# Second attention: one transfer for the turned maximum from SP's queue, rows stored tile by tile

## The chip, the cores and the metric

The kernel runs on one core of a Trainium2 chip. The metric is the time of one execution on the device in microseconds; the time before is 1258.41 us, the median of three runs (1256.88 to 1260.72).

## The reference

The input is x, 8 x 512 rows of 512 numbers, and a context of 8 x 120 rows. Four layers follow, each with a layernorm in front and a residual behind: a cross-attention with one head, a quantised linear layer, a second cross-attention with 16 heads of 32, and a mixture of experts with one shared and eight routed feed-forward networks. The change lies in the second attention:

```python
q = (query @ w_q.T).reshape(B, T_q, N_HEADS, HEAD_DIM)
k = (kv_source @ w_k.T).reshape(B, T_kv, N_HEADS, HEAD_DIM)
v = (kv_source @ w_v.T).reshape(B, T_kv, N_HEADS, HEAD_DIM)
attn = softmax(einsum('bqhd,bkhd->bhqk', q, k) * HEAD_DIM ** (-0.5), axis=-1)
out = einsum('bhqk,bkhd->bqhd', attn, v).reshape(B, T_q, D_MODEL) @ w_o.T
x = x + out
```

## The kernel before

The rows are worked on in 32 tiles of 128 (four to a batch element). The program runs four stages one after the other, each a set of five generators, one for each engine queue: the first attention with the quantised layer (`front`), the second attention (`attention1`), the shared network (`shared`) and the experts (`experts`). `both` in `stages` weaves them: the table JOIN says after which step of the first stage a part of a step of the second is issued, and the table TAIL says after which part (4 x step + part) of the second stage's last steps the first pieces of the shared network are issued.

In `attention1` a step t works on several tiles at once. TensorE makes the scores of tile t (four groups c of four heads, line L1510), and VectorE takes the maximum of each group (L1260). The maxima, split in a high and a low part (L1267, L1269), are turned by TensorE (L1517) and copied by ScalarE into `shiftT` (32 rows of 128, `shift_copied`, L1422). A transfer lays them as two more rows (96 and 97) under the packed queries of the tile, `g.queries[t % 3]`. One step later the turned scores of the tile (`scores_transposed`, L1537) are made from packed keys and packed queries with these rows, so that the maximum comes off in the same product. ScalarE's exponentials follow (L1391, L1395, L1402), GpSimd makes low parts (L1217), TensorE the outputs (L1553 to L1555), the output is turned (L1560) and goes through the output product (`product(t - 3, k)` in four quarters, L1606). The queries of tile t + 2 are made by `queries` (L124 is the helper `matmuls`).

Transfers: SP writes the queries of tile t + 1 to `q_rows` (L1184), waits until they landed, and reads them back packed with three loads (`packed_queries`, by the helper `spread`, L133). It stores the normed rows of tile t - 4 to `xn_rows` (L1188) and their turned form to `xt_tiles` (L1197). Every fourth step it stores four tiles of the residual rows to `x_rows` (L1204, 1 MB). Every fourth step it loads packed keys (also L133). ScalarE's queue issues the transfer of the turned maximum, in two halves of 4 KB (`shift_rows`, L1428), behind the exponentials of group 3. `n_in` counts these landings: TensorE waits for it ahead of the first turned scores, ScalarE ahead of the next copy.

An engine issues its instructions in the order in which the generators give them; a wait for a semaphore holds everything behind it on that engine.

## Time and profile before

| | us |
|---|---|
| median of three runs | 1258.41 |
| profiled execution | 1257.52 |
| its span | 1255.7 |
| TensorE (PE) busy | 1175.9 |
| VectorE (DVE) busy | 934.9 |
| ScalarE (ACT) busy | 664.5 |
| GpSimd (POOL) busy | 538.9 |
| second attention, some 32 tiles | about 250 to 620 |

Times in the trace are microseconds from the span's start. PEld is TensorE's weight load, which runs beside its matmuls; a name with q (SPq, ACTq) is an instruction of the engine's queue alone, such as the issue of a transfer. A number in square brackets at the end of a timeline's line is the idle time of the engine before it, with what ended it. The end of a matmul is modelled, so its start is the safer number.

### The profile page before, as it was taken

Reading aid. Unit: us, or ns where it says so; the run is one execution under the profiler, and the core shown is the slowest. Engines: PE = TensorE matmul, PEld = TensorE weight load, DVE = VectorE, ACT = ScalarE, POOL = GpSimd, SP = SyncE. Lnnn points to the kernel's source line nnn. Section 1 sums busy time; section 2 is a strip of 40 time slices with the busy share of each in tenths; the row PEclk is TensorE's granted clock in tenths of the full one; section 3 lists DMA queues with packets and bytes.
Section 4 is the critical chain, followed back from the end, with each engine's and each line's share of the span. In section 5 each row is a group of like instructions: output and inputs, shape, how many; then the busy total and the mean of one; then the engine's idle time right before and its main releaser. Section 6 shows DMA issues by size and latency. Waiting matters only on the chain.

```text
span 1255.7 us, 28634 instructions
## 1 busy us (share of the span) xinstructions
PE 1175.9 (94%) x10724; PEld 800.9 (64%) x10724; DVE 934.9 (74%) x2080; ACT 664.5 (53%) x1199; POOL 538.9 (43%) x682
## 2 busy tenths in 40 slices
PE   6888998679999999997899999999999999999996
PEld 3555655567777787875444444677777777666663
DVE  5899897878898898886586777777677776645450
ACT  4377787567788787775454322122222232465652
POOL 0057667644444444432200000364555455277744
PEclk9999999999999999999999999999999999999999
DMA  9522023123445444562791050304121503599987
GB/s 343 213 68 69 1 33 45 43 75 119 164 152 165 165 154 167 169 178 78 214 182 34 1 168 1 102 2 102 23 80 35 168 23 106 161 254 240 262 137 97
DMA packets 159608, 150.49 MB, mean 120 GB/s; under 512 B 80592, under 2 KB 113520, under 8 KB 159472
## 3 DMA queue, kind: packets, MB, share of 16 engines
q1 hardware_dynamic: 138432, 121.75, 33.6%
q0 software_dynamic: 14400, 25.35, 9.9%
q10 hardware_dynamic: 6640, 1.58, 0.7%
q8 instruction: 86, 1.41, 0.5%
q14 instruction: 50, 0.41, 0.1%
HBM read 84.93 MB, written 57.19 MB: 113 GB/s over the span
## 4 chain that ended last, share of the span: by engine, by line
PE 78%; DVE 8%; DMA 6%; issue 3%; ACT 2%; POOL 2%; ACTq 0%; SPq 0%; DVEq 0%; POOLq 0%
PE bank L124 28%; PE bank L2241 15%; PE bank L2234 13%; PE bank L1606 6%; DMA att_land<-att_land 4%; PE bank L980 3%; PE bank L1537 3%; PE bank L1560 2%; PE bank L1510 2%; PE bank L1049 1%; DMA q_rows<-att_land 1%; PE bank L897 1%; DMA att_land<-q_rows 1%; DVE front_amax L793 1%; PE bank L916 1%
## 5 line engine op out<-in xcount | busy, mean ns | idle before, releaser
L1739 POOL DMA_INDIRECT lists<-att_land x128 | 135.5, 1058 | 287.6 <-DVE att_land L1880 168.8
L2234 PE MATMUL bank<-att_land 128*128 128x512 f16 x768 | 176.2, 379 | 0.0
L124 PE MATMUL bank<-program_xs,program_wgu 128*128 128x512 f16 x576 | 128.9, 379 | 0.6 <-DVE att_land L1839 0.6
L2062 ACT ACTIVATE att_land<-program_x 128x512 f32<-128x512 f32 x40 | 25.2, 631 | 195.2 <-DVE program_x L2204 195.2
L2234 PEld LDWEIGHTS bank<-att_land 128*128 128x128 f16 x768 | 75.1, 98 | 81.7
L1217 POOL TENSOR_TENSOR att_land<-att_land 120x512 f16<-120x512 f32 x64 | 74.2, 1159 | 92.5 <-ACT att_land L1402 92.5
L124 PE MATMUL bank<-att_land 128*128 128x128 f16 (+1 forms) x1560 | 106.0, 221 | 3.0 <-DVE att_land L1323 3.0
L1260 DVE TENSOR_REDUCE bank<-bank 128x4 f32<-128x480 f32 x128 | 84.8, 662 | 30.9 <-PE bank L1510 29.5
L1606 PE MATMUL bank<-att_land 128*128 128x512 f16 x384 | 104.0, 383 | 1.7 <-DVE att_land L1344 1.7
L124 PEld LDWEIGHTS bank<-program_xs,program_wgu 128*128 128x128 f16 x576 | 56.0, 98 | 67.3 <-DVE att_land L1839 1.1
L124 PEld LDWEIGHTS bank<-att_land 128*128 128x128 f16 x1560 | 89.3, 98 | 5.9 <-DVE att_land L1323 3.5
L2241 PE MATMUL bank<-program_x 128*128 128x256 f16 x720 | 85.1, 273 | 0.0
L2403 POOL DMA_INDIRECT out_rows<-program_x,att_land x40 | 69.9, 1747 | 34.5 <-ACT program_x L2444 19.5
L124 PE MATMUL bank<-program_x 128*128 128x256 f16 (+2 forms) x504 | 80.5, 318 | 0.6 <-DVE program_x L2496 0.6
L1402 ACT ACTIVATE att_land<-bank 120x512 f16<-120x512 f32 x128 | 76.7, 599 | 8.0 <-PE bank L1537 5.0
L2013 ACT ACTIVATE att_land<-att_land 128x512 f16<-128x512 f32 x64 | 40.3, 629 | 74.2 <-PE bank L2234 34.5
L2241 PEld LDWEIGHTS bank<-program_x 128*128 128x128 f16 x720 | 70.5, 98 | 8.1
L451 POOL TENSOR_TENSOR program_x<-program_x,att_land 128x512 f32<-128x512 f32 x32 | 40.8, 1276 | 75.8 <-ACT att_land L569 75.8
L2073 DVE TENSOR_TENSOR att_land<-att_land 128x512 f16<-128x512 f32 x64 | 43.9, 686 | 33.2 <-ACT att_land L2013 33.1
L124 PE MATMUL bank<-program_wgu,att_land 128*128 128x120 f16 (+1 forms) x480 | 52.2, 253 | 16.6 <-DVE att_land L770 13.9
L124 PEld LDWEIGHTS bank<-program_x 128*128 128x128 f16 x504 | 49.2, 98 | 28.9 <-DVE program_x L2496 1.1
L2241 PE MATMUL bank<-program_xs,program_wgu 128*128 128x256 f16 x480 | 65.6, 273 | 0.0
(322 smaller groups left out, 2967.7 us busy)
## 6 DMA issues: line engine op xcount, KB each, us to landing
xn_rows<-att_land SPq DMA_DIRECT2D x37, 256.0 KB, 2.9
out_rows<-att_land SPq DMA_DIRECT2D x37, 256.0 KB, 7.2
att_land<-q_rows SPq DMA_DIRECT2D x66, 128.0 KB, 2.6
q_rows<-att_land SPq DMA_DIRECT2D x32, 256.0 KB, 2.1
xt_tiles<-att_land SPq DMA_DIRECT2D x32, 256.0 KB, 2.1
x_rows<-program_x SPq DMA_DIRECT2D x8, 1024.0 KB, 4.8
att_land<-x_rows SPq DMA_DIRECT2D x8, 1024.0 KB, 5.5
program_xs<-xt_tiles SPq DMA_DIRECT2D x28, 256.0 KB, 5.4
```

What stands on the lines that cost most here:

```text
L124: last = pe.matmul(out, lhs(a, k), rhs(b, k), start=n == 0, stop=n == len(terms) - 1)
L451: pool.tensor_tensor(g.x[:, u, :], g.x[:, u, :], y[:, u % 2], ALU.add).then_inc(a["x_new"], 1)
L1217: pool.tensor_tensor(pT[0:J, c, 1], prob[0:J, c], pT[0:J, c, 0], ALU.subtract).then_inc(c4["p_lo"], 1)
L1260: dve.tensor_reduce(nmax[:, c], ps_s[:, :, :], AX.X, ALU.max, negate=True).then_inc(c4["max"], 1)
L1402: act.activation(pT[0:J, c, 0], ps_t[c % 2][0:J, :], ACT.Exp).then_inc(c4["p_hi"], 1)
L1606: last = pe.matmul(ps_y[:, :], oT[:, u % 2, a, k, :], g.wo1[:, b, k, :], start=k == 0 and n == 0, stop=k == KC - 1 and n == 2)
L1739: pool.indirect_dma_start(out=io["lists"], out_offset=bass.IndirectOffsetOnAxis(ap=index[:, t, k:k + 1], axis=0), in_=load[:, t, k, :], in ...
L2013: act.activation(hid[:, v % 2, 0], hf[:, v % 2], ACT.Copy).then_inc(s["h_hi"].handle, 1)
L2073: tt(hid[:, v % 2, 1], hf[:, v % 2], hid[:, v % 2, 0], ALU.subtract).then_inc(s["h_lo"].handle, 1)
L2234: last = pe.matmul(ps_y[i][:, :], hid[:, c % 2, a, i * P:(i + 1) * P], wd[:, q, c, :], start=c == 0 and n == 0, stop=c == NC - 1 and n == 2)
L2241: last = pe.matmul(out, lhs(a, k), rhs(q, k), start=n == 0, stop=n == len(terms) - 1)
L2403: pool.indirect_dma_start(out=io["out"], out_offset=bass.IndirectOffsetOnAxis(ap=lst[:, u * CT + n, 0:1], axis=0), in_=res[:, c, n, :], in ...
```

## The change

Six things. On SP, the store of `xn_rows` moves from between the write of `q_rows` and the packed loads to behind these loads. The store of `x_rows` is made for each tile, in the step in which its `xn_rows` is stored, instead of for four tiles every fourth step. The transfer of the turned maximum is issued by SP behind these two, as one transfer of 32 rows, after a wait for ScalarE's copy; ScalarE's `shift_rows` is gone, and `n_in` counts 16 a tile instead of 32. On TensorE, the first turned scores (group 0) come behind the first quarter of the output product and the scores of group 1 instead of ahead of both, and the second ones (group 1) behind the third quarter instead of ahead of it. The shared network's wait for the stored rows counts 32 stores. In TAIL, the first piece of the shared network on TensorE goes in behind part 3 of step 31 instead of part 2.

```diff
--- before.py
+++ after.py
@@ -1183,9 +1183,6 @@
                 sp.wait_ge(s["q_lo"], u + 1)
                 sp.dma_start(io["q_rows"][u], qT[:, :, :, :].rearrange("p q k n -> p q (k n)")).then_inc(q_out[u % 2], 16)
             v = t - 4
-            if live(v):
-                sp.wait_ge(lg.ok, v + 1)
-                sp.dma_start(io["xn_rows"][v * P:(v + 1) * P, :], lg.xn[:, v % 2]).then_inc(rows_out[v % 2], 16)
             if live(u):
                 sp.wait_ge(q_out[u % 2], 16 * (u // 2 + 1))
                 need(sp, c4["t_mm"], KC * (u - 2))
@@ -1193,15 +1190,17 @@
                     sp.wait_ge(f.a["sim"], NT)
                 packed_queries(sp, g, io, u, q_in)
             if live(v):
+                sp.wait_ge(lg.ok, v + 1)
+                sp.dma_start(io["xn_rows"][v * P:(v + 1) * P, :], lg.xn[:, v % 2]).then_inc(rows_out[v % 2], 16)
+                sp.wait_ge(s["x_new"], v + 1)
+                sp.dma_start(io["x_rows"][v * P:(v + 1) * P, :], g.x[:, v, :]).then_inc(g.x_out.handle, 16)
+            if live(t):
+                sp.wait_ge(s["n_ok"], t + 1)
+                sp.dma_start(g.queries[t % 3][COPIES * DH:ROWS].rearrange("p r (c n) -> p (r c) n", n=P),
+                             shiftT[0:2 * HEADS, :]).then_inc(n_in, 16)
+            if live(v):
                 sp.wait_ge(s["g_lo"], v + 1)
                 sp.dma_start(io["xt_tiles"][v, :, :], gT[:, v % 2].rearrange("p q k n -> p (q k n)")).then_inc(gt_out[v % 2], 16)
-
-            if t >= TB and t % TB == 0:
-                b = t // TB - 2
-                if b >= 0:
-                    sp.wait_ge(s["x_new"], TB * (b + 1))
-                    rows = io["x_rows"][b * S:(b + 1) * S, :].rearrange("(i p) n -> p i n", p=P)
-                    sp.dma_start(rows, g.x[:, b * TB:(b + 1) * TB, :]).then_inc(g.x_out.handle, 16)
 
         def finish():
             for n in range(2):
@@ -1418,15 +1417,8 @@
         def shift_copied(u):
             if live(u):
                 act.wait_ge(s["n_mm"], u + 1)
-                need(act, n_in, 32 * u)
+                need(act, n_in, 16 * u)
                 act.activation(shiftT[0:2 * HEADS, :], ps_n, ACT.Copy).then_inc(s["n_ok"], 1)
-
-        def shift_rows(u):
-            if live(u):
-                act.wait_ge(s["n_ok"], u + 1)
-                for q in range(2):
-                    act.dma_start(g.queries[u % 3][COPIES * DH + q:COPIES * DH + q + 1].rearrange("p r (c n) -> p (r c) n", n=P),
-                                  shiftT[q * HEADS:(q + 1) * HEADS, :]).then_inc(n_in, 16)
 
         def query_high(u):
             if live(u):
@@ -1480,7 +1472,6 @@
             shift_copied(t)
             yield
             exps(t - 1, 3)
-            shift_rows(t)
             gate_high(t - 4)
             weights_high(t)
             if t == NT - 6:
@@ -1522,7 +1513,7 @@
                 return
             b = u // TB
             if c == 0:
-                pe.wait_ge(n_in, 32 * (u + 1))
+                pe.wait_ge(n_in, 16 * (u + 1))
                 if u % TB == 0 and b < 2:
                     pe.wait_ge(ones, b + 1)
             if u == 0 and c == 0:
@@ -1631,13 +1622,13 @@
         def step(t):
             scores(t, 0)
             rows_transposed(t + 2)
+            product(t - 3, 0)
+            yield
+            scores(t, 1)
             scores_transposed(t - 1, 0)
-            product(t - 3, 0)
-            yield
-            scores(t, 1)
             product(t - 3, 1)
+            product(t - 3, 2)
             scores_transposed(t - 1, 1)
-            product(t - 3, 2)
             yield
             scores(t, 2)
             product(t - 3, 3)
@@ -1963,7 +1954,7 @@
                     sp.dma_start(io["out"][bass.ds(((b - 1) * TB + i) * P, P), :], res[:, i]).then_inc(out_done.handle, 16)
             if b < B:
                 if b == 0:
-                    need(sp, g.x_out, 16 * B)
+                    need(sp, g.x_out, 16 * NT)
                     need(sp, t.y_mm, NT)
                 need(sp, out_done, 16 * TB * b)
                 sp.dma_start(res[:, :, :], io["x_rows"][b * S:(b + 1) * S, :].rearrange("(i p) n -> p i n", p=P)) \
@@ -2610,7 +2601,7 @@
         "gpsimd": [],
         "scalar": [135, 137, 142, 143],
         "vector": [135, 139, 150],
-        "tensor": [126, 130, 134, 139, 143, 147]}
+        "tensor": [127, 130, 134, 139, 143, 147]}
 
 
 def stages(nc, g, io):
```

## Rows read from the trace of the kernel before

**Rows 1.** The page's chain of work that ended last, by engine.
```profile
PE 78%; DVE 8%; DMA 6%; issue 3%; ACT 2%; POOL 2%; ACTq 0%; SPq 0%; DVEq 0%; POOLq 0%
```
**Rows 2.** Windows: length, busy time (instructions) by engine; clock, DMA share, GB/s.
```profile
454.76:464.83 10.07, 10.07 (x163) 8.53 (x161) 9.53 (x23) 8.77 (x16) 4.28 (x8) 1.00 0.49 160
443.53:454.76 11.23, 10.27 (x163) 8.50 (x161) 9.73 (x23) 8.24 (x15) 5.59 (x10) 1.00 0.50 153
```
**Rows 3.** Waits of TensorE's weight loads, 270 to 585: total, times, longest.
```profile
PEld bank L1537 <- DMA att_land<-att_land: 12.3, 11, 1.6
PEld bank L1510 <- DMA att_land<-q_rows: 5.7, 3, 2.3
...
PEld bank L1537 <- DMA program_xs<-att_land: 1.3, 2, 0.7
```
**Rows 4.** Chain of work in a stalled tile: start, length, what.
```profile
444.71 3.88 DMA att_land<-att_land
```
**Rows 5.** Timeline of a quiet tile, TensorE: start, length, what.
```profile
458.64 0.36 PEld L1537 LDWEIGHTS bank<-att_land 98*120 98x120 f16 x4
458.92 0.37 PEld L1606 LDWEIGHTS bank<-att_land 128*128 128x128 f16 x3
459.41 0.42 PEld L1510 LDWEIGHTS bank<-att_land,program_xs 96*128 96x128 f16 x4
459.78 0.37 PEld L1606 LDWEIGHTS bank<-att_land 128*128 128x128 f16 x3
...
458.75 0.39 PE L1537 MATMUL bank<-att_land 98*120 98x128 f16 x4
```
**Rows 6.** Timeline of the same tile, ScalarE and its queue.
```profile
455.03 0.27 ACT L1422 ACTIVATE att_land<-bank 32x128 f16<-32x128 f32 x1 [0.67 <-PE bank L1517]
...
455.40 0.51 ACTq L1428 DMA_DIRECT2D att_land<-att_land  x1
...
455.95 0.61 ACTq L1428 DMA_DIRECT2D att_land<-att_land  x1
457.01 0.60 ACT L1467 ACTIVATE att_land<-bank 128x512 f16<-128x512 f32 x1 [0.53 <-PE bank L1560]
...
459.44 0.59 ACT L1391 ACTIVATE att_land<-bank 120x512 f32<-120x512 f32 x1
```
**Rows 7.** Timeline of the same tile, VectorE.
```profile
458.50 0.67 DVE L1260 TENSOR_REDUCE bank<-bank 128x4 f32<-128x480 f32 x1 [0.16 <-PE bank L1510]
```
**Rows 8.** Timeline of SP's queue, the next step.
```profile
459.84 0.34 SPq L1184 DMA_DIRECT2D q_rows<-att_land  x1
...
461.88 1.28 SPq L133 DMA_DIRECT2D att_land<-q_rows  x3
468.43 0.34 SPq L1197 DMA_DIRECT2D xt_tiles<-att_land  x1
468.81 0.43 SPq L1204 DMA_DIRECT2D x_rows<-program_x  x1
```
**Rows 9.** DMA issues: the turned maximum's landing; then size and median to landing.
```profile
DMA to landing us min/median/max: 1.7/2.1/4.3
...
att_land<-q_rows SPq DMA_DIRECT2D x66, 128.0 KB, 2.6
```
**Rows 10.** Chain of work: writes of q_rows that landed late.
```profile
469.91 4.10 DMA q_rows<-att_land
...
535.55 6.53 DMA q_rows<-att_land
...
557.36 5.35 DMA q_rows<-att_land
```
**Rows 11.** Window behind the last of these (columns as in rows 2).
```profile
570.00:574.00 4.00, 4.00 (x23) 2.38 (x22) 2.29 (x7) 1.60 (x3) 2.21 (x2) 0.65 0.56 198
```
**Rows 12.** Waits of TensorE's weight loads, 562 to 625 (columns as in rows 3).
```profile
PEld bank L1537 <- DMA att_land<-att_land: 1.4, 1, 1.4
```
**Rows 13.** Timeline of ScalarE at the stage's end.
```profile
587.82 0.60 ACT L1402 ACTIVATE att_land<-bank 120x512 f16<-120x512 f32 x1 [2.66 <-PE bank L1537]
```

More of the change, by code:

```diff
@@ L1633, in step @@
             rows_transposed(t + 2)
-            scores_transposed(t - 1, 0)
             product(t - 3, 0)
@@ L1637, in step @@
             scores(t, 1)
+            scores_transposed(t - 1, 0)
             product(t - 3, 1)
+            product(t - 3, 2)
             scores_transposed(t - 1, 1)
-            product(t - 3, 2)
             yield
```

## The prediction

> **What bounds the kernel now.** I read the page's chain of work first, then the waits of TensorE's weight loads over the second attention, then one stalled and one quiet tile of that stage in the timelines. The chain is TensorE for 78% and DMA for 6% [rows 1], so what the change is worth is the part of that DMA share which TensorE waits for. In the second attention (270 to 585 us) two lines of TensorE wait for transfers [rows 3]: L1537, the turned scores, for the turned maximum (12.3 us in 11 waits and 1.3 in 2, together 13.6 in 13, mean 1.05, longest 1.6), and L1510, the scores, for the packed queries (5.7 us in 3). A tile without such a wait lasts 10.07 us, with TensorE busy for 10.07, VectorE for 9.53 and ScalarE for 8.77; the tile before it waited and lasted 11.23 [rows 2]. So the bound of a quiet tile is TensorE itself, VectorE has 0.54 us to spare, and a wait is paid in full. In the stalled tile the second of the two transfers landed 3.88 us after its issue [rows 4], against 2.1 in the median and 1.7 at best [rows 9]: it met other traffic.
>
> **The change part by part.**
> *The turned maximum.* Before, ScalarE copies it until 455.30 (455.03 + 0.27), its sequencer issues two transfers at 455.40 and 455.95 [rows 6], and the weight load that needs both starts at 458.64 [rows 5]: 3.34 us after the copy. The one transfer from SP can go as early as the first of the two, 0.55 sooner than the second, if SP is free. In the next tile SP issues the three packed loads from 461.88 to 463.16 [rows 8]; the two stores that now follow (0.34 to 0.43 each by the same rows) bring it to about 464.0, over 1 us ahead of that tile's copy (10.07 us after 455.30, so 465.4). SP thus waits for the copy. Behind that wait stand the store of xt_tiles, which went at 468.43, some 3 us later, and the next tile's q_rows; neither is held.
> *TensorE's order.* The first turned scores go behind one quarter of the output product and the second scores: 458.64 to 458.92 is their own place, 458.92 to 459.41 the product's, 459.41 to 459.78 the scores' [rows 5]. So they start 0.49 + 0.37 = 0.86 later, 4.20 us after the copy. Both together loosen the bond by 0.86 + 0.55 = 1.41 against a mean wait of 1.05 and a longest of 1.6. Of the 13.6 us I let 1.5 stay for single late landings; the ends are 0 and, if the transfer lands no sooner than the second did and each wait were the longest, 13 x (1.6 - 0.86) = 9.6. Gain 12.1.
> *What that order costs.* The second scores come 0.28 sooner (458.64 to 458.92 falls out ahead of them), at 459.13, while the maximum they wait for ends at 459.17 (458.50 + 0.67) [rows 7]. I put 0.05 us a tile for it, over 28 tiles 1.4; ends 0 and 3. ScalarE's first exponential waits for the moved scores: their products end at 459.14, so 460.00 now, and it starts about 0.60 behind the 459.44 of before [rows 5, 6]. The cover is ScalarE's idle 0.67 ahead of the copy of the maximum [rows 6]: 0.07 is left, cost nothing. Without that cover it is 0.60 a tile. GpSimd's low parts move by as much and stay off the chain.
> *ScalarE's issues.* 64 issues of 0.51 to 0.61 us leave its sequencer; the next activation waits 0.53 for TensorE anyway [rows 6], so this is worth nothing in the middle of the stage. At its end it counts: the last tile's issue stands behind an activation that waits 2.66 us for TensorE [rows 13], because a unit of the next stage was put ahead of that, and TensorE then waits 1.4 [rows 12]. The change moves that unit one part later (126 to 127) and issues from SP: 1.2 gained, ends 0 and 1.4.
> *x_rows tile by tile.* Before, one store of 1 MB goes every fourth tile right ahead of a q_rows write [rows 8]. That write then took 4.10 and 5.35 us to land [rows 10], against 2.0 in a quiet tile (459.84 issued, 461.88 the loads that wait for it [rows 8]), and the packed loads behind it came late: two of the three waits of L1510. The third, behind the 6.53 us write [rows 10], falls where ScalarE loads tokens and stays. Now 256 KB goes behind the packed loads, out of the write's way. Gain: the 2.3 us wait [rows 3] and one of about 1.5, 3.8 in all, and part of what the slow clock took after the longer one (granted share 0.65 over 4 us [rows 11], so up to 1.4): I take 1.1. Together 4.9; ends 0 and 3.8 + 1.4 = 5.2 (5.7 + 1.4 with the third). Moving xn_rows behind the packed loads costs nothing: its buffer is wanted again two tiles later. 24 more issues of about 0.4 us lie in SP's idle time.
> *The sum:* -12.1 - 4.9 - 1.2 + 1.4 = -16.8. The profiled execution took 1257.52 (span 1255.7 and 1.8 around it), so 1240.7; it lies 0.9 under the median of 1258.41, so 1241.6 for the median. All later stages follow TensorE's chain and are carried along.
>
> **A rule against the change.** The traced transfers of 4 KB land in 2.1 us in the median, and 128 KB of packed loads in 2.6 [rows 9]; no row shows a transfer shaped as the new one (2 partitions on one side, 32 on the other). The Trainium skill, DMA: Bandwidth & Descriptors, section "Why a DMA increments its semaphore by 16 and not by 1", says that a transfer runs on the largest number of engines up to 16 that divides the slowest dimension of both sides: here 2, where each of the old ones had 16. By it each of the two engines moves 4 KB, half of what one engine has of a packed load, so it would land about as late as one of these, 0.5 us past 2.1, and the sum would keep all but a little of its 12.1; where other traffic shares those two engines it is the first rival.
>
> **The rivals.**
> 1. *The transfer lands later than the second of the two did,* because it queues behind two 256 KB stores on SP's queue or because one transfer of 8 KB takes longer than one of 4 KB. If it lands 0.5 later than the second in the 13 loaded tiles, 13 x (1.05 - 0.86 + 0.5) = 9.0 of the waits stay instead of 1.5: 1249.1. For it: the loaded landings of 3.88 [rows 4]. Against it: over 1 us between SP's last store and the copy, and 1.41 of slack. (The rule above from the Trainium skill would work in this direction.)
> 2. *The packed queries stay late,* since the bytes of x_rows still cross each tile and only the burst is gone. Then the 4.9 falls out: 1246.5.
> 3. *ScalarE's cover isn't there,* for instance because the second exponential is late as well, and the 0.60 is paid in 28 tiles, 16.8: 1258.4, no change. Against it: 8.77 + 0.53 + 0.60 = 9.90 of 10.07 [rows 2, 6].
> 4. *Slower: the turned maximum always lands behind the stores on SP's queue,* as q_rows did behind x_rows. With the 5.35 us of that row [rows 10] from an issue 0.1 after the copy it lands 5.45 after it, and 5.45 - 4.20 = 1.25 is waited for in each of 28 tiles, 35.0 instead of 1.5: 1275.1. It decides from a landing of about 4.85 us after the copy on (18.3 / 28 = 0.65 a tile), which now only loaded tiles come near. Against it: 0.5 MB a tile and not 1 MB at once, issued over 1 us earlier.
>
> **How the numbers follow.** Forecast 0.63, rival 1 0.15, rival 2 0.11, rival 3 0.05, rival 4 0.06. The forecast's own range runs from all waits gone with nothing paid (13.6 + 5.7 + 1.4 + 1.4 = 22.1, so 1236.3) to some 3 us above it. With rivals 1 and 2 the range is 1236.3 to 1249.5, which leaves out rivals 3 and 4 and the far ends of the first. A measurement of this kernel tells about 0.3%, 4 us, from no change: faster 0.89 (forecast, rivals 1 and 2), same 0.05 (rival 3), slower 0.06 (rival 4).
>
> **What would show it.** In the profile after: waits of L1537's weight loads for the turned maximum under 3 us in all; waits of the scores for packed queries only near the tokens' load; quiet tiles of 10.07 to 10.15; ScalarE's idle time ahead of the copy near 0.1; the last turned maximum issued right behind its copy. A tile longer than 10.4 without a named transfer would make the step on ScalarE wrong; a median landing above 4 us the step on SP's queue.

## The result, and the profile after

The changed kernel takes 1241.12 us in the median (1238.86 to 1245.78), the kernel before 1258.62 in the same series: a ratio of 0.9865, 95% interval 0.983 to 0.990. The forecast was 1241.6 with a range of 1236.3 to 1249.5. So the time is right; the experiments below show that the reason given for it is right only in part.

The profiled execution has a span of 1241.1 us. The first fence is the chain of work by engine, which answers [rows 1]; the second holds the waits of TensorE's weight loads from 270 to 575 us, as in [rows 3] (total, times, longest).

```profile
PE 84%; DVE 8%; issue 3%; ACT 2%; POOL 1%; DMA 1%; ACTq 0%; SPq 0%; DVEq 0%; POOLq 0%
```
```profile
PEld bank L1501 <- DVE bank L1259: 7.9, 29, 2.9
...
PEld bank L1501 <- DMA program_xs<-q_rows: 0.5, 1, 0.5
```

DMA fell from 6% of the chain to 1%. The turned scores, L1528 now, wait for no transfer in this stretch of this execution (13.6 us in 13 waits before [rows 3]), and the scores, L1501 now, wait 0.5 us for packed queries (5.7 before). What L1501 waits for is the maximum from VectorE, 0.16 us in most tiles and once 2.9.

Where the time went by place: the second attention of both kernels in five stretches, of before and then of after. The cuts are TensorE's turning of the maximum in tiles 0, 3, 26, 28 and 31, and the first down-projection of the next stage (columns as in [rows 2]).

```profile
249.70:282.86 33.16, 26.71 (x397) 22.25 (x395) 25.68 (x55) 20.96 (x40) 14.65 (x20) 0.95 0.25 73
282.86:528.30 245.44, 233.88 (x3685) 194.77 (x3684) 220.78 (x504) 197.63 (x359) 117.51 (x198) 1.00 0.48 158
528.30:552.30 24.00, 20.85 (x325) 16.94 (x323) 17.97 (x41) 16.81 (x31) 9.69 (x14) 1.00 0.64 163
552.30:584.63 32.33, 27.76 (x405) 21.64 (x403) 25.00 (x58) 20.75 (x39) 9.96 (x15) 0.95 0.35 124
584.63:622.06 37.43, 32.34 (x289) 18.90 (x290) 19.06 (x43) 17.91 (x31) 8.38 (x20) 1.00 0.50 171
sum 372.36, PE 341.54 PEld 274.50 DVE 308.49 ACT 274.06 POOL 160.20; mean PE 68.31 PEld 54.90 DVE 61.70 ACT 54.81 POOL 32.04
```
```profile
249.98:284.01 34.03, 27.76 (x398) 23.14 (x396) 25.73 (x55) 20.98 (x40) 14.64 (x20) 0.90 0.22 69
284.01:515.43 231.42, 230.97 (x3685) 195.08 (x3683) 218.07 (x504) 195.84 (x359) 117.62 (x198) 1.00 0.51 169
515.43:541.29 25.86, 23.08 (x324) 19.42 (x322) 18.15 (x41) 16.96 (x32) 9.69 (x14) 0.87 0.67 185
541.29:569.94 28.65, 26.31 (x405) 20.72 (x403) 24.86 (x58) 20.68 (x40) 9.95 (x15) 1.00 0.41 144
569.94:607.28 37.34, 33.66 (x289) 19.15 (x290) 18.80 (x43) 17.69 (x31) 8.38 (x20) 0.95 0.44 151
sum 357.30, PE 341.79 PEld 277.50 DVE 305.61 ACT 272.15 POOL 160.27; mean PE 68.36 PEld 55.50 DVE 61.12 ACT 54.43 POOL 32.05
```

The stage is 15.06 us shorter: 14.02 in tiles 3 to 25 (TensorE busy for 230.97 of 231.42, where 11.6 us were idle before) and 3.68 in tiles 28 to 30. Two stretches grew: the first tiles by 0.87 and tiles 26 and 27 by 1.86. The last stretch stayed (37.43 and 37.34). All that follows the stage takes 633.8 us against 633.6 before.

Tile 26 is the new loss: it alone takes 15.80 of the 25.86. In ScalarE's timeline of after, the four loads of the next stage's tokens (L1100) keep its sequencer from 517.82 to 522.32, and the next activation waits 3.20 us for nothing but that issue; TensorE's third scores, which need what follows from it, start at 524.97. Part of this loss belongs to this one execution: in e3, e7 and e8 below, which have the same queue and the same order, tiles 26 and 27 take 24.3, 24.3 and 23.6 us, against 24.0 in before.

```profile
517.82 0.59 ACTq L1100 DMA_DIRECT2D program_xs<-xt_tiles  x1
518.18 1.05 ACT L1415 ACTIVATE program_wgu<-att_land 128x1024 f16<-128x1024 f32 x1
518.45 3.87 ACTq L1100 DMA_DIRECT2D program_xs<-xt_tiles  x3
522.42 0.60 ACT L1427 ACTIVATE att_land<-bank 128x512 f16<-128x512 f32 x1 [3.20 <-issue]
```

### The profile page after: what moved, and what is told of

Its sections match the earlier page's. It is cut to its first block, busy times and chain, and to the rows that moved or that the text cites. A ratio compares the mean times of both kernels' runs of the same rounds, so it can differ in the third digit from the quotient of the medians.

```text
span 1241.1 us, 28626 instructions
## 1 busy us (share of the span) xinstructions
PE 1176.2 (95%) x10724; PEld 803.1 (65%) x10724; DVE 932.9 (75%) x2080; ACT 662.7 (53%) x1199; POOL 539.2 (43%) x682
## 4 chain that ended last, share of the span: by engine, by line
PE 84%; DVE 8%; issue 3%; ACT 2%; POOL 1%; DMA 1%; ACTq 0%; SPq 0%; DVEq 0%; POOLq 0%
PE bank L124 30%; PE bank L2232 15%; PE bank L2225 13%; PE bank L1597 6%; PE bank L980 3%; PE bank L1551 3%; PE bank L1528 2%; PE bank L1501 2%; PE bank L1049 1%; PE bank L897 1%; PE bank L1546 1%; PE bank L1544 1%; PE bank L1545 1%; PE bank L916 1%; DVE front_amax L793 1%
## 5 line engine op out<-in xcount | busy, mean ns | idle before, releaser
L2225 PE MATMUL bank<-att_land 128*128 128x512 f16 x768 | 176.2, 379 | 0.0
L1597 PE MATMUL bank<-att_land 128*128 128x512 f16 x384 | 98.7, 381 | 1.7 <-DVE att_land L1343 1.7
```

What stands on the lines that cost most here:

```text
L1597: last = pe.matmul(ps_y[:, :], oT[:, u % 2, a, k, :], g.wo1[:, b, k, :], start=k == 0 and n == 0, stop=k == KC - 1 and n == 2)
L2225: last = pe.matmul(ps_y[i][:, :], hid[:, c % 2, a, i * P:(i + 1) * P], wd[:, q, c, :], start=c == 0 and n == 0, stop=c == NC - 1 and n == 2)
```

## The experiments

The change has four separable parts: how many transfers bring the turned maximum, whose queue issues them, TensorE's order, and the stores of rows. A fifth, the first piece of the shared network behind part 3 of step 31 (place 127 in TAIL, 126 before), is in every kernel of the table that issues from SP, except e11, and in no other; e11 gives its price. The table sets out all kernels by the four; a ratio is always to the kernel before on the same chip, so ratios can be compared where medians of different chips can't.

| kernel | transfers | queue | order | rows | median us | ratio (95%) |
|---|---|---|---|---|---|---|
| after | 1 | SP | new | moved | 1241.12 | 0.9865 (0.983 to 0.990) |
| e1 | 1 | SP | old | moved | 1245.72 | 0.9906 (0.988 to 0.993) |
| e2 | 2 | ScalarE | new | old | 1247.95 | 0.9926 (0.990 to 0.995) |
| e3 | 1 | SP | new | x_rows in fours | 1241.07 | 0.9867 (0.983 to 0.990) |
| e5 | 2 | SP | old | moved | 1260.50 | 0.9989 (0.996 to 1.002) |
| e6 | 1 | ScalarE | old | old | 1248.06 | 0.9898 (0.986 to 0.993) |
| e7 | 1 | SP | new | xn_rows back | 1242.22 | 0.9831 (0.978 to 0.989) |
| e8 | 1 | SP | new | old | 1244.84 | 0.9877 (0.981 to 0.994) |
| e9 | 2, by columns | ScalarE | old | old | 1257.62 | 0.9970 (0.995 to 0.999) |
| e10 | 1 | ScalarE | old | moved | 1240.07 | 0.9828 (0.979 to 0.986) |
| e12 | 2, weights' load later | ScalarE | old | old | 1269.24 | 1.0077 (1.005 to 1.010) |
| e4 | after, tokens spread | | | | 1238.72 | 0.9843 (0.981 to 0.987) |
| e11 | e4, unit at 126 | | | | 1239.51 | 0.9819 (0.978 to 0.986) |

**e1: the change with TensorE's old order.**
```diff
+            scores_transposed(t - 1, 0)
             product(t - 3, 0)
             yield
             scores(t, 1)
-            scores_transposed(t - 1, 0)
             product(t - 3, 1)
-            product(t - 3, 2)
             scores_transposed(t - 1, 1)
+            product(t - 3, 2)
```


> The changed kernel with TensorE's old order (first turned scores ahead of the product's quarter and of the second scores); the transfer from SP, the rows tile by tile and the tail stay. The bond then is 3.4 us after ScalarE's copy instead of 4.26. Theory (both loosen the bond, 0.55 by the earlier issue and 0.86 by the order): of the 13.6 us of waits of the turned scores, those longer than 0.55 come back in part, 13 x (1.05 - 0.55) = 6.5 us in all, so some 1247 to 1248. Rival a (the transfer from SP lands later than the second of the two did): waits of 13 us and more, 1254 or slower. Rival b (the early issue alone removes the waits, the order only costs): waits under 1 us and the overlap with the first stage shorter, 1240 or faster.

The waits for the transfer in this kernel, 270 to 585 us:
```profile
PEld bank L1528 <- DMA att_land<-att_land: 2.2, 1, 2.2
```
(The "bond" of the expectation is the time from the end of ScalarE's copy to the weight load that needs the transfer.) One wait is left where 6.5 us were expected, without the slack that the order gives, so in this profile the order is not needed for the 13.6 us to go. But it is the fastest of five executions (1239.81; the others took 1245.46 to 1246.16), and what the others lost is in no profile; the ratio is about the one that the 6.5 us would have given. Whether the order is worth something beside the rest the ratios don't tell, 0.9906 against 0.9865 with intervals that overlap. The wait that stays is in tile 15: SP issued 0.78 us after the copy, and GpSimd's load of weights had been issued 0.45 us after it.

**e2: the kernel before with the new order alone** (the lines of e1 the other way round).

> The kernel before with TensorE's new order alone; ScalarE's two transfers, the four-tile store and the old tail stay. Theory: each wait of the turned scores is shortened by 0.86, from a mean of 1.05 in 13 tiles to some 3 us in all; the waits for packed queries (5.7 us) stay, and the last tile's too: 1258.6 - 10.6 + 0 to 1 = 1248 to 1249. Rival (the order costs ScalarE more than its cover, or only moves the wait): quiet tiles of 10.4 and more, 1255 or slower.

The order alone gives 0.9926, about as expected:
```profile
PEld bank L1510 <- DMA att_land<-q_rows: 2.1, 1, 2.1
PEld bank L1537 <- DMA att_land<-att_land: 1.7, 3, 1.0
PEld bank L1510 <- DMA program_xs<-q_rows: 0.8, 2, 0.4
```
The 1.0 is the last tile's; in tiles 3 to 26 the turned scores wait 1.0 us in all where they waited 13.6. Two things do this. One is slack: in tiles 3, 7, 10, 16 and 23 the second transfer lands as late as before (3.9 to 4.5 us after the copy, before 3.9 to 4.5), and the weight load comes 4.26 us after the copy in a quiet tile, not 3.34. The other is GpSimd's load of weights (512 KB, every third tile). Before, it is issued 0.26 to 0.47 us after the copy in tiles 6, 9, 12, 15, 18, 21 and 24, between the two transfers. Here it is issued 1.05 to 1.08 us after the copy, behind both, because GpSimd's low parts ahead of it follow ScalarE's exponentials, which the order delays. In tile 18 of e2 (copy until 436.72):
```profile
436.83 0.51 ACTq L1428 DMA_DIRECT2D att_land<-att_land  x1
437.37 0.61 ACTq L1428 DMA_DIRECT2D att_land<-att_land  x1
```
```profile
437.77 0.61 POOL L1223 DMA_DIRECT2D att_land<-in_sh_guT  x1 [0.30 <-POOL program_wgu L1231]
```
In these seven tiles the second transfer lands 2.40 to 2.92 us after the copy, against 4.22 to 4.94 before. e9 takes the load up.

**e5: e1 with two transfers of 16 rows, from SP.**
```diff
-                sp.dma_start(g.queries[t % 3][COPIES * DH:ROWS].rearrange("p r (c n) -> p (r c) n", n=P),
-                             shiftT[0:2 * HEADS, :]).then_inc(n_in, 16)
+                for q in range(2):
+                    sp.dma_start(g.queries[t % 3][COPIES * DH + q:COPIES * DH + q + 1].rearrange("p r (c n) -> p (r c) n", n=P),
+                                 shiftT[q * HEADS:(q + 1) * HEADS, :]).then_inc(n_in, 16)
```


> The kernel after, with TensorE's order of before, and the turned maximum brought from SP's queue in two transfers of 16 rows again. The run with the old order and one transfer had 2.6 us of waits of the first turned scores in two tiles. Theory a (what made the landings late was the form of the transfer: each half is spread over more DMA engines and ends with the busiest of them): the waits come back although SP issues early, 6 us or more over the stage, the kernel before's 13.6 as the upper end; time 1245 to 1253. Theory b (the early issue from SP is all that counts): the second half is issued one issue of some 0.6 us later than the single transfer was, and only the tiles that were within 0.6 us of waiting now wait; 2 to 5 us in all, time 1240 to 1246.

```profile
PEld bank L1529 <- DMA att_land<-att_land: 15.8, 12, 3.5
PEld bank L1529 <- DMA program_xs<-att_land: 4.5, 5, 1.5
```
The waits are all back (20.3 us, more than theory a's upper end), and the time is that of before. SP issued the first half 0.03 us after the copy in most tiles and the second 0.58: SP's queue by itself brings nothing, nor do the moved stores beside it. The single transfer brings 0.8% against this kernel (e1). Two halves from SP with the new order were not run.

**e6: the kernel before with one transfer, from ScalarE's queue.**
```diff
-                for q in range(2):
-                    act.dma_start(g.queries[u % 3][COPIES * DH + q:COPIES * DH + q + 1].rearrange("p r (c n) -> p (r c) n", n=P),
-                                  shiftT[q * HEADS:(q + 1) * HEADS, :]).then_inc(n_in, 16)
+                act.dma_start(g.queries[u % 3][COPIES * DH:ROWS].rearrange("p r (c n) -> p (r c) n", n=P),
+                              shiftT[0:2 * HEADS, :]).then_inc(n_in, 16)
```


> The kernel before, with one change: ScalarE's queue brings the turned maximum in one transfer of 32 rows and not in two of 16. Theory a (the form of the transfer made the late landings): the stalls of the first turned scores fall from 13.6 us to 3 or less, and the time to 1245 to 1248. Theory b (the late issue from ScalarE's queue is what counts): the single transfer is issued where the first half was, so it lands about 0.55 us before the second half did; the four or five tiles that waited 2.4 to 3.9 us still wait 2 to 3, 8 to 11 us in all, and the time is 1253 to 1257.

```profile
PEld bank L1509 <- DMA program_xs<-q_rows: 2.6, 2, 2.3
PEld bank L1509 <- DMA att_land<-q_rows: 2.1, 2, 1.3
```
No wait of the turned scores is left, with the old queue and the old order. What is left are the packed queries, 4.7 us; this profiled execution was the fastest of its eight (1241.08), so the median of 1248.06 holds more of something that this profile doesn't show.

**e9: two transfers, cut by columns.** A packet count tells the form of a transfer. The queue q10 carries ScalarE's transfers in these three kernels. Its packets (number, MB, share) and the issues (size, landing) around one tile of before, of e6 and of e9:
```profile
q10 hardware_dynamic: 64, 0.01, 0.8%
...
att_land<-in_sh_guT POOLq DMA_DIRECT2D x1, 512.0 KB, 3.9
...
att_land<-att_land ACTq DMA_DIRECT2D x2, 4.0 KB, 2.8
```
```profile
q10 hardware_dynamic: 34, 0.01, 0.6%
...
att_land<-att_land ACTq DMA_DIRECT2D x1, 8.0 KB
```
```profile
q10 hardware_dynamic: 68, 0.01, 0.9%
...
att_land<-att_land ACTq DMA_DIRECT2D x2, 4.0 KB
```
Each half of 16 rows sends 16 pieces and 16 counts, one for each engine (2 x 32 = 64). The single transfer sends 32 pieces and 2 counts: it runs on two engines. Two halves by columns send 2 x (32 + 2), two engines each. So e9 keeps the second issue and removes the spread.
```diff
-                    act.dma_start(g.queries[u % 3][COPIES * DH + q:COPIES * DH + q + 1].rearrange("p r (c n) -> p (r c) n", n=P),
-                                  shiftT[q * HEADS:(q + 1) * HEADS, :]).then_inc(n_in, 16)
+                    act.dma_start(g.queries[u % 3][COPIES * DH:ROWS].rearrange("p r (c n) -> p (r c) n", n=P)[:, :, q * (P // 2):(q + 1) * (P // 2)],
+                                  shiftT[0:2 * HEADS, q * (P // 2):(q + 1) * (P // 2)]).then_inc(n_in, 16)
```


> The kernel before, with the turned maximum still in two transfers from ScalarE's queue, but cut by columns: each brings 64 of the 128 columns of all 32 rows (128-byte pieces) and not 16 of the rows. In the trace of before a half of 16 rows leaves one 256-byte packet on each of 16 engines, and the late ones run behind the 4096-byte packets of the 512 KB load on POOL's queue; the one transfer of 32 rows left its packets on about two engines. A half by columns should also go to about two. Theory a (a transfer that is spread over all engines ends with the busiest, so the spread makes it late): the stalls of the first turned scores stay away, 3 us or less over the stage against 13.6, time 1245 to 1250. Theory b (the second transfer is issued some 0.55 us later and falls behind the big load whatever engines it takes; the single transfer only came early enough): 6 us or more of stalls, time 1254 to 1262.

```profile
PEld bank L1537 <- DMA att_land<-att_land: 8.3, 7, 1.5
```
By its numbers theory b came, but not in every tile. The seven waits are those of tiles 6, 9, 12, 15, 18, 21 and 24, the tiles in which GpSimd issues the 512 KB load of the next layer's weights. Before, six of these waited, 7.5 us, but tiles 3, 7, 10, 13, 16 and 23 as well, 5.4 us (the rest of the 13.6 is tile 26, where the tokens are loaded and a fetch, as described below, runs as well); here those six don't. So there are two causes, and each has its own tiles.

*The load.* In tile 18 of before (copy until 444.06), the two issues of ScalarE and the one of GpSimd:
```profile
444.17 0.51 ACTq L1428 DMA_DIRECT2D att_land<-att_land  x1
444.71 0.61 ACTq L1428 DMA_DIRECT2D att_land<-att_land  x1
```
```profile
444.52 0.61 POOL L1223 DMA_DIRECT2D att_land<-in_sh_guT  x1 [0.30 <-POOL program_wgu L1231]
```
The load is issued between the halves. The packet records of the trace show it: the first half's pieces go from 445.35 on, the load's 4 KB packets from 445.82, and the second half's pieces run at 447.5 to 448.0, when the load's are nearly through. The single transfer of e6 was issued 0.10 to 0.15 us after the copy, and its last piece ran 1.60 to 1.94 us after it in tiles 3 to 25, mostly before the load's first packet (1.77 to 1.85). Once it meets the load, two engines don't help it: in tile 15 of e1 and of e10 its last piece ends 5.1 and 5.2 us after the copy.

*The instruction fetch.* In the other tiles a packet of 16 KB on the queue of instructions starts just as the second half's pieces go. The window of tile 13 of before:
```profile
q8 instruction: 1, 0.02, 1.9%
q10 hardware_dynamic: 64, 0.01, 1.2%
```
From the packet records of before, in us from the end of the copy:
```
tile   16 KB instruction packet   last piece of the second half   wait of L1537
3      2.01 to 3.17               3.16                            1.26
7      2.07 to 3.39               3.38                            1.12
10     1.98 to 2.97               2.96                            0.73
13     1.94 to 3.28               3.27                            1.01
16     1.97 to 2.96               2.96                            0.68
23     1.92 to 2.88               2.87                            0.60
19     2.73 to 4.02               2.07                            none
22     4.18 to 5.57               2.06                            none
```
Fifteen of sixteen pieces go at 1.9 to 2.1; one goes at the moment when the fetch ends. The records don't name the engine, so that this piece sits behind the fetch on the same engine is inferred, from six tiles in which its time and the fetch's end agree within 0.02 us. In e9 the fetch runs at the same time (1.93 to 3.05 in tiles 3, 7, 10, 13 and 16), and a half on two engines isn't touched by it.

**e12: the kernel before with the weights' load one step later.**
```diff
             ln.inverse_root(pool, g, t + 4, t % 4)
+            if 4 <= t < 4 + 3 * B and t % 3 == 1:
+                weights_in((t - 1) // 3 - 1)
             yield
...
-            if 3 <= t < 3 + 3 * B and t % 3 == 0:
-                weights_in(t // 3 - 1)
```


> The kernel before, with one change on GpSimd: the 512 KB load of the second layer's weights (every third tile) is issued one step later, behind the rows' inverse roots, some 3 us after the place where it started between the two transfers of the turned maximum. Theory a (in the tiles 3, 6, 9 to 24 the second transfer lands late because its packets queue behind this load; in the tiles after them, 7, 10, 13 and 16, because a 16 KB instruction fetch holds one of the 16 engines): the stalls of tiles 3, 6, 9, 12, 15, 18 and 24 go, 8 us or more, and those of 7, 10, 13 and 16 stay; 4 to 6 us of 13.6 are left, time 1248 to 1253, unless the load now delays the packed queries by as much. Theory b (the second transfer is late for a reason of its own on ScalarE's queue): stalls of 11 us or more, spread over the same tiles, time 1255 to 1261.

```profile
PEld bank L1510 <- DMA program_xs<-q_rows: 15.1, 6, 2.8
PEld bank L1510 <- DMA att_land<-q_rows: 2.4, 1, 2.4
PEld bank L1537 <- DMA program_xs<-att_land: 1.8, 4, 1.0
PEld bank L1537 <- DMA att_land<-att_land: 1.5, 1, 1.5
```
The time is outside both ranges; what stands behind theory a's "unless" was the larger part. In tiles 6, 9, 12, 15, 18, 21 and 24 no wait for the turned maximum is left, and the second transfer lands 2.40 to 2.87 us after the copy (4.22 to 4.94 before): the load was their cause. Tile 3, which the expectation counted among them, still waits 1.5 us, beside a fetch, as tile 23 does (1.0). But now the load runs into the write of q_rows. In the chain of work the longest of these writes takes 7.16 us:
```profile
387.85 7.16 DMA q_rows<-att_land
```
The 1 MB store of x_rows stands ahead of that one too; two writes with the load alone, for tiles 11 and 17, took 6.28 and 6.33 us, and 2.26 and 2.00 before. The packed loads wait for these writes and TensorE for them, 17.5 us in all, and the kernel is 0.8% slower than before. What becomes of tiles 7 to 16 can't be read here: their turned scores start later anyhow.

**e3, e7, e8 and e10: the rows.** e3 puts only x_rows back into fours, e7 only xn_rows back ahead of the packed loads, e8 both; e10 is e6 with both moved as in after.
```diff
# e3, e8
-                sp.wait_ge(s["x_new"], v + 1)
-                sp.dma_start(io["x_rows"][v * P:(v + 1) * P, :], g.x[:, v, :]).then_inc(g.x_out.handle, 16)
...
+            if t >= TB and t % TB == 0:
+                b = t // TB - 2
+                if b >= 0:
+                    sp.wait_ge(s["x_new"], TB * (b + 1))
+                    rows = io["x_rows"][b * S:(b + 1) * S, :].rearrange("(i p) n -> p i n", p=P)
+                    sp.dma_start(rows, g.x[:, b * TB:(b + 1) * TB, :]).then_inc(g.x_out.handle, 16)
# e7, e8: ahead of the packed loads
+            if live(v):
+                sp.wait_ge(lg.ok, v + 1)
+                sp.dma_start(io["xn_rows"][v * P:(v + 1) * P, :], lg.xn[:, v % 2]).then_inc(rows_out[v % 2], 16)
```


> The changed kernel with x_rows stored four tiles at a time as before (1 MB at the end of every fourth step, ahead of the next q_rows write). Theory: the q_rows writes of these steps land 4 to 5 us after issue, one or two waits for packed queries of 1.5 to 2.5 us come back, and the clock falls after the longer: 4 to 5 us slower than the changed kernel, 1245 to 1246. Rival (with the waits of the turned maximum gone and xn_rows behind the loads, the loads have room even behind 1 MB): no wait of over 0.5 us comes back, same as the changed kernel, 1241.

> The kernel after, with the store of xn_rows put back between the q_rows write and the loads of the packed queries; x_rows is still stored tile by tile behind them. Theory a (what removed the waits for packed queries, 3.8 us before, is that xn_rows no longer stands in between): second scores and transposes wait 2 to 4 us again in some two or three tiles, time 1243 to 1246. Theory b (either the rows tile by tile or xn_rows behind the loads is enough): waits for the packed queries under 1 us in all, time 1240 to 1243.

> The kernel after with all stores of rows as before: xn_rows between the q_rows write and the packed loads, x_rows in fours at the end of the step; the new order and the turned maximum from SP's queue stay. With x_rows in fours alone nothing was lost. Theory a (the move of xn_rows carries this part of the gain): waits for the packed queries of 2 to 4 us with 1 us of slow clock behind them, time 1244 to 1247. Theory b (these waits come and go with the phase of the transfers and none of the stores of rows carries them): within 1 us of the kernel after, and the part of the prediction that credited 4.9 us to the rows has no cause in this stage at all.

> The kernel before, with one transfer of 32 rows from ScalarE's queue and with the stores of xn_rows and x_rows moved as in the kernel after (tile by tile, behind the packed loads); SP does not bring the turned maximum and TensorE keeps its old order. Theory a (the number of transfers and the place of the rows are all of the gain; SP's queue and the new order add nothing): stage as long as in the kernel after, 357 us, waits for the packed queries under 1.5 us, time 1240 to 1244. Theory b (SP's issue or the order still carries a part): as with one transfer alone, waits for the packed queries of 3 to 5 us, stage 358.7 us or longer, time 1244 to 1249.

With SP and the new order the rows make no difference that can be told: 0.9867, 0.9831 and 0.9877 against 0.9865. With ScalarE's queue and the old order they do: e6 0.9898, e10 0.9828, intervals that only touch, and where the runs of e6 reach from 1241 to 1254, those of e10 lie between 1238 and 1243. In the profiles with x_rows in fours (before, e2, e3, e6, e8, e9; e12 apart) the q_rows write behind each of these stores lands after 4.0 to 5.9 us; the packed loads then come up to 1.5 us ahead of their use or up to 2.9 behind it. It is a near thing that falls either way: 5.7, 2.9, under 0.2, 4.7, 1.0 and 2.9 us of waits. With x_rows tile by tile (after, e1, e4, e5, e7, e10, e11) it is 0 to 1.5. e10's expectation a holds in time (1240 to 1244), though not in its stage (359.2 us): tile 15 lost 4.1 us, where the single transfer met the load after all.

**e4 and e11: the tile that grew.** e4 gives ScalarE one token load in each of steps 23 to 26 and not four in step 26; e11 also puts TensorE's unit back to 126.
```diff
-            if t == NT - 6:
...
-                tokens(act, g, io, 0, 0, xs_in)
+            i = t - (NT - 6 - TB + 1)
+            if 0 <= i < TB:
...
+                src = io["xt_tiles"][i, :, :].rearrange("p (a n) -> p a n", n=P)
+                act.dma_start(g.xs[:, 0, :, :, i * P:(i + 1) * P].rearrange("p q k n -> p (q k) n"), src).then_inc(xs_in, 16)
# e11 as well
-        "tensor": [127, 130, 134, 139, 143, 147]}
+        "tensor": [126, 130, 134, 139, 143, 147]}
```


> The changed kernel with ScalarE's four token loads for the shared network issued one in each of steps 23 to 26 instead of all four in step 26. Theory: the 15.8 us tile of step 26 comes from ScalarE's sequencer, which issues for 4.5 us while the next activation, the q_rows write behind it and TensorE's third scores wait, and from the slow clock behind that wait; spread, each issue of about 0.6 to 1.1 us lies beside an activation, the tile falls to 10.1 to 10.6 and the time by 5 to 6 us, to 1235 to 1236. Rival (it is the megabyte of the loads on the DMA engines, not the issue): q_rows writes land late in four steps instead of one, and the gain is under 2 us.

> The kernel after with ScalarE's four loads of the next stage's tokens spread over steps 23 to 26 (this alone gave a stage of 353.5 us) and TensorE's first piece of the next stage put at place 126 as before, not 127. If the place of that piece costs the tail: the time from the last tile to the next stage falls from 37.6 us to 36.3 and the run to 1236 to 1238. If the last tile's end hangs on the same exponentials at either place: the same as with the tokens spread alone, 1238 to 1240.

In e4 the long tile is gone, as expected: tiles 26 and 27 take 20.12 us. The time fell less than the 5 to 6 us expected: 0.9843 against 0.9865 of after, with intervals that overlap. The last three of the five stretches in e11:
```profile
517.34:537.46 20.12, 20.12 (x324) 17.03 (x323) 17.90 (x41) 16.87 (x32) 9.69 (x14) 1.00 0.62 191
537.46:566.11 28.65, 26.30 (x405) 20.72 (x403) 24.85 (x58) 20.70 (x40) 9.95 (x15) 1.00 0.42 145
566.11:602.45 36.34, 32.28 (x289) 18.90 (x290) 18.99 (x43) 17.71 (x31) 8.39 (x20) 1.00 0.44 154
```
Tiles 26 and 27 take 20.12 us, TensorE busy throughout, against 25.86 in after and 23.6 to 24.3 in e3, e7 and e8. The tail takes 36.34 against 37.34, and 37.65 in e4: its 289 matmuls are the same, but at 127 they took 33.66 us at a mean granted clock of 0.95 (part of the stretch at the lower level, 1.2 GHz), here 32.28 at 1.00. All profiles divide like this: with the unit at 127 (after, e1, e3, e4, e5, e7, e8) the tail takes 37.3 to 37.7 us at a granted clock of 0.95, with it at 126 and one transfer (e6, e10, e11) 36.1 to 36.3 at 1.00. The stage is 352.3 us long against 357.3 of after. The time, 1239.51, lies in the range of the expectation's second case, though the tail did what the first one says. By the times e11 is faster than before by 1.4 to 2.2%; the interval overlaps that of after, with which it was not timed on one chip, so that it beats the changed kernel rests on the profile alone.

## Why the prediction was right, and where it was not

*The waits for the turned maximum, -12.1.* The place and the size held: 13.6 us of waits are gone and tiles 3 to 25 are 14.02 shorter, of which 1.57 is a packed-query wait in tile 21. The 1.5 that I let stay is there in other executions: e4 and e11, which are the kernel after up to tile 22, wait 1.4 and 1.5 us in tile 15, and their stretch is 12.3 shorter than that of before.

The mechanism held in part. I took the late landings as given and set 0.55 us from one issue in place of two and 0.86 from TensorE's order, as slack, against a mean wait. The order's slack is real and measures 0.92 (3.34 to 4.26), but it explains only the tiles of the fetch; in those of the load the order works by moving the load behind both transfers (e2), a delay of GpSimd that I had down as free. The 0.55 alone should have left 6.5 us, and e6's profile has none: the single transfer goes ahead of the load, and on two engines the fetch doesn't hold it. SP adds nothing to this. Its issue is hardly earlier than ScalarE's first one was (0.03 against 0.11 after the copy), and with two halves it gains nothing (e5). It is the second transfer that was late. I had read "it met other traffic" from the 3.88 us of [rows 4] and didn't ask which traffic, and why it met the second half. The answer was in the trace of before: the load issued 0.19 us ahead of it, and the fetch. One transfer alone (e6) or the order alone (e2) takes away nearly all of these waits in its profile; the kernel after has both, and how its gain divides between them is open.

*The rule weighed.* I took the form of the new transfer, two engines in place of 16, for a danger: 0.5 us later. The Trainium skill, DMA: Bandwidth & Descriptors, section "Why a DMA increments its semaphore by 16 and not by 1", is right on the number of engines, and the 2 counts in e6 agree. The price drawn from it was on the wrong side. The last piece of the single transfer (e6) runs 1.6 us after the copy in a quiet tile, that of the second half at 2.05 to 2.08. And with two engines it has fewer queues to be stuck in: in e9's profile that is worth the 5.4 us of the fetch's tiles. Rival 1, in whose favour the rule spoke, fell.

*TensorE's order, +1.4.* In quiet tiles it costs nothing: the weight load of the second scores waits 0.16 us for the maximum, three times my 0.05, but behind matmuls that still run. Tile 20 of after lasts 10.06 us against 10.07 [rows 2], TensorE busy throughout.

```profile
455.07:465.13 10.06, 10.06 (x163) 8.51 (x161) 9.51 (x23) 8.80 (x17) 5.08 (x9) 1.00 0.44 148
```
It does cost something where the stage begins beside the first attention. Counted from the start of the span, tile 3 begins 1.2 us later in after than in before (284.01 and 282.86, of which 0.87 falls in the stage's first tiles, at a granted clock of 0.90 against 0.95). Of two pairs that differ in the order alone, it begins 1.3 us later in e2 than in before, and 4.6 later in after than in e1. With one transfer it begins at 279.5 to 281.3 under the old order (e1, e6, e10) and at 283.3 to 286.2 under the new (after, e3, e4, e7, e8, e11). These are single executions, but they agree: the sign of the term came, at a place that I had not priced. How the order does it was not followed up. ScalarE's idle time ahead of the copy went from 0.67 to 0.14, near the 0.07 that I had, so rival 3 fell as argued. What the order buys beside SP is slack, since SP is sometimes late, and a later load: in tile 15 SP issues 0.8 us after the copy in both e1 and after, in e1 behind the load (2.2 us of wait), in after ahead of it (1.05, none). In after's tile 19 the copy ends at 444.96, but SP still waits 4.4 us for a q_rows write, then issues the packed loads and two stores, and the turned maximum goes 2.07 us late:
```profile
439.90 0.41 SPq L1184 DMA_DIRECT2D q_rows<-att_land  x1
444.78 1.26 SPq L133 DMA_DIRECT2D program_xs<-q_rows  x3
446.08 0.43 SPq L1194 DMA_DIRECT2D xn_rows<-att_land  x1
446.56 0.43 SPq L1196 DMA_DIRECT2D x_rows<-program_x  x1
447.03 0.62 SPq L1199 DMA_DIRECT2D att_land<-att_land  x1
```
My "over 1 us ahead of the copy" came from one quiet tile. ScalarE's queue has nothing of the kind ahead of it. So the move to SP and the new order are two parts that pay for each other; e10, without either, is as fast as after, and faster than e1 with SP alone (0.9828 against 0.9906, intervals apart).

*The tail, -1.2.* It was 0.09. The last turned maximum is issued at once, as I had it, and its wait of 1.4 us [rows 12] is gone. But the other half of the same edit, the unit at 127, costs 1.3 (e4 37.65, e11 36.34), by a slower clock over the tail; I had priced only its gain. Nor was the unit's move needed: with one transfer and the unit at 126 the wait is gone too, and the tail takes 36.1 (e6, e10).

*x_rows tile by tile, -4.9.* The 5.7 us of waits did fall to 0.5, and tiles 28 to 30 gained 3.68. As a step it is too sure of itself: e3, with x_rows in fours, has the same time and the same 28.65 us in tiles 28 to 30, while e6 against e10, which moves both stores, shows 0.7% (some 9 us). What it removes is a wait that comes and goes by a few tenths of a microsecond; its price lies between 0 and about 9, and one profile couldn't give it. Why the fours do so little harm once SP brings the turned maximum and the order is new is left open.

*The tokens' tile, "stays".* It grew by 1.86 in this execution, though not in e3, e7 and e8. The wait of the packed queries that I left there is gone, but the third scores wait 2.9 us where they waited 1.5: the same four issues kept ScalarE's sequencer for 3.4 us before (530.69 to 534.05) and keep it for 4.5 now. I had carried a wait over without asking what it hung on. Why the same issues take longer is open.

*The sum.* In the profiled executions: -14.02 - 3.68 - 0.09 + 0.87 + 1.86 = -15.06 for the stage, against -16.8; -17.0 by the ratio of the medians. Misses of both signs met: no cost in quiet tiles and all 13.6 us gone on one side, the tail and the tokens on the other. That the median came within 0.5 us of the forecast is luck to that extent. Rivals 2 and 4 fell: the packed queries wait 0.5 us in all, and the turned scores for no transfer at all.

## What to carry to other kernels

When a small transfer sometimes lands late, list by tile what else is issued in the same microsecond, on every queue, before pricing a new order or another queue: here one merged transfer from the old queue gave what three edits were credited with, and an order that seemed to buy slack also moved another engine's load. A transfer waited for as a whole is as late as its latest piece; here one issue on two engines was safer than two issues on sixteen. A queue that also carries waits for other data is a poor place for the one transfer on the critical path, and moving a large load out of one transfer's way can put it into another's, which may be the dearer one: 0.6 us later (e2) it was in nobody's, 3.5 us later (e12) in that of the q_rows write.

## What the runs showed of the hardware

An instruction fetch is a 16 KB packet of 0.9 to 1.7 us in the second attention of before; in six tiles of before the last of 16 pieces of a 4 KB transfer ran as it ended. The Trainium skill, Runtime: NRT & Kernel Launch, section "Instruction fetch mechanics", gives the 16 KiB blocks and calls their cost mostly hidden; for the fetching engine no run here shows otherwise, but in these six tiles TensorE waited 0.6 to 1.3 us for another queue's transfer.

A 512 KB load on GpSimd's queue holds back a 4 KB transfer issued 0.2 us behind it by some 2 us (its last piece ends 3.7 to 4.4 us after the copy and not at 2.1). Where the load is issued 0.4 us behind the transfer, as in e2, the piece ends at 2.1. In e12 a 256 KB write of q_rows beside the load took 6.3 us, against 2.0 in a quiet tile [rows 8].

Four loads of 256 KB on ScalarE's queue kept its sequencer for 4.5 us in one tile of after, 0.6 to 1.8 us each (3.4 us before), with activations standing behind them; one a tile took 0.53 to 0.60 each (e4, e11) and cost nothing that the tile lengths show (10.06 us).
